# Token-expert layers of an eight-layer hybrid model: weights split once and kept in DRAM, spreading matrix by ScalarE, routing in halves, early tiles between late ones

## The chip, the cores and the metric

One core of one Trainium2 chip runs the whole kernel in one launch. The metric is the device time of one execution in microseconds; the median of the runs is compared. Engines are named as in the profile: PE (TensorE; PEld is its weight load), DVE (VectorE), ACT (ScalarE), POOL (GpSimd), SP (SyncE, which issues the DMAs).

## The reference

The model takes x of 4 x 512 tokens of 128 floats and adds eight layers to it, each on a layer norm of x: attention with a learned position bias, expert-choice experts, linear attention, experts again, a selective scan, the token-expert layer, a delta-rule layer, and the token-expert layer once more with the same weights. The token-expert layer is what this case is about:

```python
scores = jax.nn.sigmoid(x @ gate_weight.T)          # 32 experts in 4 groups
sc = scores + gate_bias                             # best 2 groups by their two best scores, best 6 experts in them
tw = tw / (tw.sum(-1, keepdims=True) + 1e-20) * 0.2 # weights of the 6
g, u = einsum('th,ehi->tei', x, w_gate), einsum('th,ehi->tei', x, w_up)
routed = sum over experts of cw * (silu(g) * u) @ w_down
shared = silu(x @ shared_w_gate) * (x @ shared_w_up) @ shared_w_down
anchor = one of 16 small experts, chosen by the best expert
out = routed + shared + 0.1 * anchor
```

All experts are computed for all tokens; the routing enters as a weight per token and expert. Inputs and outputs are float32.

## The kernel before

The kernel runs the layers one after the other, each as a block with five instruction streams. At a block's end all engines meet, so a layer starts when the one before is finished. The first layer is `layer_attention` (tag la), the sixth and eighth are `layer_moe_tokens` (tags lf and lh).

**The token layer.** The hidden columns of all experts stand side by side: 16 tiles of 128 columns for the 32 routed experts, 4 for the 16 anchors, 1 for the shared expert, which makes 21 tiles. The tokens are 4 chunks of 512. A unit is one tile of one chunk, so there are 84. Products are in fp32r, and to keep float32's accuracy weights and activations are split into a high and a low part, so each product is three matmuls (high by high, high by low, low by high).

*Head of the layer.* SP loads the raw weights in order anchors and shared, routed, then the down weights, which overwrite the raw gate weights and so wait until these are split. POOL builds a matrix `spread` of zeros and ones that spreads an expert's weight over its hidden columns (a memset and four affine selects), then splits the weights: three pieces of gate and up, then the down weights, each with a cast (L1554, L1563) and a subtraction (L1558, L1565). DVE normalises the tokens (L125), PE turns them (L136), ACT copies them out of PSUM twice (L1578, L1579), DVE subtracts the low part of the activations (L1626). PE makes the router's logits (L1735), ACT the sigmoid (L1581). Then DVE routes all 16 token tiles in one chain of small instructions (L1630 to L1689), of which nearly each waits for the one before. Meanwhile PE computes three early tiles, the last two anchor tiles and the shared one, for all chunks (12 units), and ACT keeps their silu and up parts (L1585, L1586). When the routing is done PE turns the routing weights (L1748), ACT copies them (L1589), and the main loop starts.

*Main loop.* For a late unit PE makes gate (three matmuls into bank 0 or 1), up (three into bank 2 or 3) and the spread weights (one into bank 4 or 5); ACT takes silu of the gate (L1611); DVE multiplies it by up (L1712) and by the spread weight (L1715); ACT rounds the result to its high part (L1596); POOL subtracts the low part (L1570); and two units later (LAG) PE makes the three down matmuls, which add into bank 6. An early unit has no gate and up matmuls: PE has one spread and three down matmuls in it (the shared tile three alone), while DVE, ACT and POOL have nearly the work of a late unit. The three early units stand at the end of each chunk. The rings of hidden values have 3 places. After each chunk ACT copies bank 6, PE turns it back (L1790) and DVE adds it to x (L1695).

**The attention layer.** It runs 16 groups (4 heads of one batch) in a software pipeline of 8 steps per group. PE, DVE (L434) and ACT work on every step; POOL copies the operands of group n into `stack` (L317) after it has copied the values of group n-2 (L325), which waits for PE's products of an older group. SP loads the position bias of each set of heads in turn (L268, L273), behind waits for DVE and for PE's scores.

## Time and profile before

| | us |
|---|---|
| median of 3 runs (1806.40 to 1813.23) | 1809.97 |
| the profiled execution | 1810.92 |
| its span, first to last instruction | 1807.4 |
| attention layer la, first to last DMA issue of the next layer | 7.4 to 344.7 |
| token layer lf | 1094.2 to 1347.9 |
| token layer lh | 1548.2 to 1801.9 |

PE is busy for 80% of the span, DVE for 68%, POOL for 42%, ACT for 40%; the DMA queue that SP feeds moved 31.21 MB in 6.6% of the 16 DMA engines' span. The rows that the prediction uses are in a section of their own below. Times are microseconds from the start of the span, and L numbers are lines of the kernel before.

### The profile page before, as it was taken

How to read it: one execution, taken by the hardware profiler on the slowest of the kernel's cores; microseconds unless marked ns; L12 is line 12 of the kernel's file. 1: busy time of each engine (PE TensorE's matmuls, PEld its weight loads, DVE VectorE, ACT ScalarE, POOL GpSimd, SP SyncE). 2: the span in 40 equal slices, each digit the busy share in tenths (PEclk: the TensorE clock that was granted, in tenths of full speed). 3: DMA queues.
4: the chain of work that ended last, by engine and by line, in shares of the span. 5: the costliest groups of instructions: out<-in, count | busy, mean ns of one | idle time of the engine just before them, and what ended most of it. 6: DMA issues, size and time to landing. Idle time of an engine off the chain costs nothing. (4 is left out here: it accounts for less than half of the span.)

```text
span 1807.4 us, 26498 instructions
## 1 busy us (share of the span) xinstructions
PE 1441.0 (80%) x9238; PEld 953.1 (53%) x9238; DVE 1232.8 (68%) x2834; ACT 727.1 (40%) x1218; POOL 751.0 (42%) x928
## 2 busy tenths in 40 slices
PE   4899999849965499785898886699974784669997
PEld 2333333428843278634665655476752583547775
DVE  5777777375567745667998997766667636876665
ACT  2277777511121212365443423344435111244443
POOL 3821220037510286003665656355561330635555
PEclk9599999969988699887999996799997797579999
DMA  1220100001100001100000003100000000310000
GB/s 52 64 80 19 59 2 1 25 0 36 35 11 23 2 24 37 27 1 0 1 1 1 1 1 61 30 1 1 0 7 1 0 1 1 61 30 1 1 1 24
DMA packets 39333, 32.70 MB, mean 18 GB/s; under 512 B 13856, under 2 KB 33392, under 8 KB 39216
## 3 DMA queue, kind: packets, MB, share of 16 engines
q1 hardware_dynamic: 39216, 31.21, 6.6%
q8 instruction: 65, 1.06, 0.2%
q14 instruction: 52, 0.43, 0.1%
HBM read 29.99 MB, written 1.21 MB: 17 GB/s over the span
## 5 line engine op out<-in xcount | busy, mean ns | idle before, releaser
L434 DVE CUSTOM_DVE_ANT_1 la_neg<-bank,la_table 128x512 f32<-128x512 f32 x256 | 166.5, 688 | 45.8 <-PE bank L525 45.2
L1712 DVE SCALAR_TENSOR_TENSOR xn<-xn,bank 128x512 f32<-128x512 f32 x144 | 99.0, 687 | 140.0 <-PE bank L1727 139.2
L1362 PEld LDWEIGHTS bank<-le_diag,le_dtxT 128*128 128x128 f32 x1024 | 126.3, 191 | 80.5 <-issue 59.1
L1362 PE MATMUL bank<-le_diag,le_dtxT 128*128 128x128 f32 x1024 | 141.8, 282 | 25.4 <-DVE le_h L1280 21.2
L1280 DVE TENSOR_TENSOR_SCAN le_h<-le_keep,bank 128x512 f32<-128x512 f32 x128 | 155.2, 1213 | 3.8 <-PE bank L1362 3.8
L1611 ACT ACTIVATE xn<-bank 128x512 f32<-128x512 f32 x144 | 86.1, 598 | 167.3 <-PE bank L1727 166.8
L1570 POOL TENSOR_TENSOR lf_h_low<-lf_wu,lf_h_high 128x512 fp32r<-128x512 f32 x84 | 109.2, 1301 | 90.4 <-ACT lf_h_high L1596 90.4
L1570 POOL TENSOR_TENSOR lh_h_low<-lh_wu,lh_h_high 128x512 fp32r<-128x512 f32 x84 | 109.3, 1301 | 90.3 <-ACT lh_h_high L1596 90.3
L1218 ACT ACTIVATE le_keep<-le_dt,le_A 128x512 f32<-128x512 f32 x128 | 92.1, 722 | 133.1 <-DVE le_h L1280 133.1
L361 ACT ACTIVATE la_probT<-bank 128x512 f32<-128x512 f32 x256 | 135.6, 605 | 13.4 <-PE bank L544 11.4
L1133 POOL TENSOR_TENSOR le_hc<-le_hc 128x512 f32<-128x512 f32 x64 | 81.0, 1266 | 101.7 <-DVE le_hc L1289 97.9
L1141 POOL TENSOR_TENSOR le_diag<-ident,le_bT 128x512 f32<-128x512 f32 x64 | 71.2, 1135 | 71.3 <-ACT le_bT L1205 70.4
L1289 DVE TENSOR_TENSOR le_hc<-le_h,bank 128x512 f32<-128x512 f32 x128 | 85.4, 668 | 9.4 <-issue 5.0
L325 POOL COPY la_v<-xn 128x128 f32<-128x128 f32 x16 | 4.8, 298 | 185.1 <-PE bank L555 185.1
L544 PE MATMUL bank<-la_bias_parts,la_spread 96*32 96x512 bf16 x1024 | 80.5, 392 | 0.0
L47 PE MATMUL bank<-ident 128*128 128x512 bf16 x100 | 29.9, 467 | 57.0 <-DVEq L738 40.4
L525 PE MATMUL bank<-la_qkT 48*128 48x512 bf16 x256 | 66.6, 412 | 5.5 <-DVE la_nmax L434 5.2
L555 PE MATMUL bank<-la_probT,la_v 128*32 128x512 f32 x512 | 67.5, 602 | 3.7 <-ACT la_mixT L374 3.5
L683 POOL TENSOR_SCALAR lb_pick<-lb_number,lb_own 128x128 bf16<-128x128 f32 x120 | 70.1, 610 | 0.8
L683 POOL TENSOR_SCALAR ld_pick<-ld_number,ld_own 128x128 bf16<-128x128 f32 x120 | 69.9, 609 | 0.8
L1924 POOL TENSOR_TENSOR lg_cT<-lg_aT,lg_masks 128x512 f32<-128x512 f32 x24 | 30.1, 1268 | 91.9 <-DVE lg_aT L2006 61.8
L1374 PE MATMUL bank<-le_hc,ident 128*128 128x512 f32 x128 | 65.7, 594 | 2.5 <-POOL le_hc L1133 2.5
(603 smaller groups left out, 3726.6 us busy)
## 6 DMA issues: line engine op xcount, KB each, us to landing
la_table<-la_scratch SPq DMA_DIRECT2D x4, 1792.0 KB, 7.1
la_bias_parts<-la_scratch_parts SPq DMA_DIRECT2D x12, 248.0 KB, 6.2
lb_w1s<-in_L_ffn_w_dram SPq DMA_DIRECT2D x8, 256.0 KB, 2.7
lb_w2s<-in_L_ffn_w_dram SPq DMA_DIRECT2D x8, 256.0 KB, 3.3
ld_w1s<-in_L_ffn_w_dram SPq DMA_DIRECT2D x8, 256.0 KB, 2.8
ld_w2s<-in_L_ffn_w_dram SPq DMA_DIRECT2D x8, 256.0 KB, 3.1
out_dram<-x SPq DMA_DIRECT2D x1, 1024.0 KB, 5.1
le_win<-in_L_attn_a_w_in_dram SPq DMA_DIRECT2D x1, 256.0 KB, 2.6
```

The source lines that it names most:

```text
L361: act.activation(probT[:, u % NPT, :], k.bank[RING1 + u % RING2][:], ACT.Exp).then_inc(exped, 1)
L434: dve.tensor_tensor_reduce(out=neg[:, u % 2, :].rearrange("p (c i) -> p c i", i=P), in0=k.bank[u % RING1][:].rearrange("p (c i) -> p c i", ...
L544: last = pe.matmul(k.bank[RING1 + u % RING2][i * CG:(i + 1) * CG, :], spread[:], bias_parts[:, n // B % 2, 2 * hp + e, w:w + T], start=Fal ...
L683: last = pool.tensor_scalar(pick[:, s, j, :], number[:], own[:, s, j:j + 1], None, ALU.is_equal)
L1133: pool.tensor_tensor(hc[:, p % PAIRS, 0, :], hc[:, p % PAIRS, 0, :], hc[:, p % PAIRS, 1, :], ALU.add).then_inc(paired, 1)
L1218: act.activation(keep[:, q % UN, :], dt_[:, c, g * G2 + bb, :], ACT.Exp, scale=A[:, c, n:n + 1]).then_inc(keep_ready, 1)
L1280: dve.tensor_tensor_scan(h[:, i, :], keep[:, i, :], k.bank[4 + q % 2][:], 0.0, ALU.mult, ALU.add).then_inc(scanned, 1)
L1289: dve.tensor_tensor(hc[:, p % PAIRS, n % 2, :], h[:, q % UN, :], k.bank[6 + n % 2][:], ALU.mult).then_inc(hc_ready, 1)
L1362: last = pe.matmul(k.bank[4 + q % 2][:, j * P:(j + 1) * P], dtxT[:, (g * G2 + bb) * TPB + j, c, :], diag[:, d % DIAGS, j, :], start=True, ...
L1570: pool.tensor_tensor(h_low[:, u % RING, :], hidden[:, u % RING, :], h_high[:, u % RING, :].bitcast(F32), ALU.subtract)\
L1611: act.activation(silu[:, v % 2, :], k.bank[v % 2][:, :], ACT.Silu).then_inc(silu_ready, 1)
L1712: dve.scalar_tensor_tensor(gated[:, n % 2, :], sl, 1.0 if t < ET else ALPHA, up, ALU.mult, ALU.mult).then_inc(gated_ready, 1)
```

## The change

One class `TokenWeights` is new. It declares six DRAM tensors, high and low parts of the gate, up and down weights, each 128 x 2688 floats (8.26 MB together). They are filled in the attention layer, in nine pieces of 7 tiles (896 columns): SP loads a piece, POOL casts it and subtracts, SP stores both parts. The pieces are loaded, split and stored in two slots; POOL splits piece i between groups, ahead of its copies for group n = 5 + i; SP issues the loads and stores behind its bias loads of the second, third and fourth set of heads, and waits for the last store before the layer ends.

Each token layer then loads the finished parts straight into their tiles, early columns first, the late columns in two halves, the down weights last, and splits nothing. POOL's only work in the head is the memset of `spread`; ACT fills it with four copies from the identity matrix, one ahead of its square root and three behind the copies of the turned tokens. PE turns the router's weights first and then runs 14 idle products, ahead of the turning of the tokens. DVE subtracts the low part of the activations from PSUM. The logits wait for each group of four turned tiles by itself.

The routing is a generator, called for 8 token tiles at a time with buffers of half the size. The first half runs ahead of the main loop; the second gives one small piece after each unit, up to unit 29, and its stack is turned at units 30 and 33. The order of tiles in a chunk is six late, one early, six late, one early, six late, the shared tile. LAG is 3 and the ring has 4 places. The hidden values and the chunk sums have buffers of their own.

The diff, cut to its core:

```diff
+class TokenWeights:
+    TILES_OF_PIECE = 7
+    PIECE = TILES_OF_PIECE * P
+    PIECES = 9
...
+        self.high = [nc.dram_tensor(f"token_{w}_high", [P, 3 * self.PIECE], F32) for w in ("gate", "up", "down")]
+        self.low = [nc.dram_tensor(f"token_{w}_low", [P, 3 * self.PIECE], F32) for w in ("gate", "up", "down")]
...
@@ layer_attention, SyncE @@
+            def load_piece(i):
+                if i >= 2:
+                    sp.wait_ge(piece_split, i - 1)
+                for place, source in weights.pieces[i]:
+                    sp.dma_start(place(split_raw[:, i % 2, :]), source).then_inc(piece_loaded[i % 2], 16)
+            def store_piece(i):
+                which, at = weights.place(i)
+                sp.wait_ge(piece_split, i + 1)
+                sp.dma_start(weights.high[which][:, at], split_high[:, i % 2, :].bitcast(F32)).then_inc(piece_stored[i % 2], 16)
+                sp.dma_start(weights.low[which][:, at], split_low[:, i % 2, :].bitcast(F32)).then_inc(piece_stored[i % 2], 16)
...
+                if g == 1:
+                    load_piece(0)
+                    load_piece(1)
+                if g >= 2:
+                    for i in (range(0, 4) if g == 2 else range(4, PIECES)):
+                        store_piece(i)
+                        if i + 2 < PIECES:
+                            load_piece(i + 2)
+            for slot in range(2):
+                sp.wait_ge(piece_stored[slot], 32 * len(range(slot, PIECES, 2)))
...
@@ layer_attention, GpSimd @@
+            def split_piece(i):
+                raw, high, low = split_raw[:, i % 2, :], split_high[:, i % 2, :], split_low[:, i % 2, :]
+                if weights.pad(i) is not None:
+                    link(pool.memset(weights.pad(i)(raw), 0.0))
+                pool.wait_ge(piece_loaded[i % 2], 16 * (loads_before(i) + len(weights.pieces[i])))
+                if i >= 2:
+                    pool.wait_ge(piece_stored[i % 2], 32 * (i // 2))
+                pool.tensor_copy(high, raw).then_inc(piece_high, 1)
+                pool.wait_ge(piece_high, i + 1)
+                pool.tensor_tensor(low, raw, high.bitcast(F32), ALU.subtract).then_inc(piece_split, 1)
...
+                if 5 <= n < 5 + PIECES:
+                    pool.wait_ge(v1_ready, n - 1)
+                    split_piece(n - 5)
...
@@ layer_moe_tokens @@
-    RING, LAG = 3, 2
+    GB, RING, LAG = 2, 4, 3
     U = B * TILES
+    HALF = NT // 2
+    ORDER = [t for i in range(EARLY) for t in (*range(i * LATE // EARLY, (i + 1) * LATE // EARLY), LATE + i)]
+    NO_WEIGHT = ORDER.index(TILES - 1)
...
+        SECOND_TURNS = {TILES + 9: 2, TILES + 12: 3}
+        SECOND_DUE = TILES + 8
...
@@ SyncE @@
+            for dst, src in ((wu_high, weights.high[1]), (wu_low, weights.low[1]), (wg_high, weights.high[0]), (wg_low, weights.low[0])):
+                sp.dma_start(dst[:, early_columns].bitcast(F32), src[:, early_columns]).then_inc(loaded_early, 16)
+            sp.dma_start(gb[:], gate_bias.partition_broadcast(P)).then_inc(loaded_gb, 16)
+            for columns in (slice(0, LATE // 2 * P), slice(LATE // 2 * P, LATE * P)):
+                for dst, src in ((wg_high, weights.high[0]), (wg_low, weights.low[0]), (wu_high, weights.high[1]), (wu_low, weights.low[1])):
+                    sp.dma_start(dst[:, columns].bitcast(F32), src[:, columns]).then_inc(loaded_late[columns.start > 0], 16)
+            for dst, src in ((wd_high, weights.high[2]), (wd_low, weights.low[2])):
+                sp.dma_start(dst[:].rearrange("p t d -> p (t d)").bitcast(F32), src[:, :]).then_inc(loaded_down, 16)
...
@@ GpSimd @@
-            link(pool.memset(wg[:, TILES * P - (P - SI):], 0.0))
-            link(pool.memset(wu[:, TILES * P - (P - SI):], 0.0))
...
-            for part in range(3):
-                v = spread[:, 0:ET * P].rearrange("r (e i) -> r e i", i=I)
-                link(pool.affine_select(out=v, in_=v, compare_op=ALU.not_equal, fill=1.0, base=-E * part,
-                                        pattern=[[-1, E], [0, I]], channel_multiplier=1))
...
-            for n, (t0, t1) in enumerate(((LATE, TILES), (0, LATE // 2), (LATE // 2, LATE))):
-                piece = slice(t0 * P, t1 * P)
-                if n == 1:
-                    pool.wait_ge(loaded_in, 16 * NI)
-                for raw, high in ((wu, wu_high), (wg, wg_high)):
-                    last = pool.tensor_copy(high[:, piece], raw[:, piece])
-                last.then_inc(high_ready, 1)
-                pool.wait_ge(high_ready, n + 1)
-                for raw, high, low in ((wu, wu_high, wu_low), (wg, wg_high, wg_low)):
-                    last = pool.tensor_tensor(low[:, piece], raw[:, piece], high[:, piece].bitcast(F32), ALU.subtract)
-                last.then_inc(low_ready, 1)
...
-            pool.wait_ge(loaded_w, 16 * NW)
-            pool.tensor_copy(wd_high[:], wd).then_inc(wd_ready, 1)
-            pool.wait_ge(wd_ready, 1)
-            pool.tensor_tensor(wd_low[:], wd, wd_high[:].bitcast(F32), ALU.subtract).then_inc(wd_ready, 1)
+            pool.memset(spread[:], 0.0).then_inc(cleared, 1)
...
@@ ScalarE @@
+            def make_spread(part):
+                n, columns = (E, slice(0, ET * P)) if part < 3 else (L, slice(ET * P, (ET + AT) * P))
+                rows = slice(E * part, E * part + n)
+                act.activation(spread[rows, columns].rearrange("r (e i) -> r e i", e=n), bcast(k.ident16[rows, E * part:E * part + 1], (1, n), (0, columns.stop // n - columns.start // n)), ACT.Copy)\
+                   .then_inc(spread_made, 1)
+            act.wait_ge(cleared, 1)
+            make_spread(0)
...
+            for part in range(1, 4):
+                make_spread(part)
...
+            for c in range(2):
+                copy_stackT(c)
+            for u in range(LAG):
+                silu(u)
...
@@ VectorE @@
-                dve.tensor_tensor(x_low[:, xg], k.xnT[:, xg], x_high[:, xg].bitcast(F32), ALU.subtract).then_inc(x_low_ready, 1)
-            dve.wait_ge(loaded_gw, 32)
+                dve.tensor_tensor(x_low[:, xg], k.bank[g][:], x_high[:, xg].bitcast(F32), ALU.subtract).then_inc(x_low_ready, 1)
...
+            def route(half):
+                tokens = slice(half * HALF, (half + 1) * HALF)
+                own = score[:, tokens, :]
...
+            for _ in route(0):
+                pass
+            second = route(1)
...
+                if u < SECOND_DUE:
+                    next(second, None)
+                if u == SECOND_DUE:
+                    for _ in second:
+                        pass
...
@@ TensorE @@
+            k.idle_products(pe, 14, 4)
...
+            pe.wait_ge(loaded_early, 64)
...
-            pe.wait_ge(stack_ready, 1)
-            for j in range(NT):
-                g, o = 6 + j // 8, j % 8
-                last = pe.transpose(k.bank[g][0:STK, :].bitcast(BF16)[:, o * P:(o + 1) * P], stack[:, j, :], k.ident16[:])
-                if o == 7:
-                    last.then_inc(stack_turned, 1)
-            pe.wait_ge(stackT_ready, 2)
-            pe.wait_ge(wd_ready, 2)
-            pe.wait_ge(early_kept, EARLY * B)
-            pe.wait_ge(spread_made, 7)
...
+            def turn_stack(c):
+                pe.wait_ge(stack_ready, c // 2 + 1)
+                if c == 2:
+                    pe.wait_ge(acc_used, 1)
+                if c == 3:
+                    pe.wait_ge(stackT_ready, 3)
+                for j in range(TPB):
+                    last = pe.transpose(turned_stack(c)[:, j * P:(j + 1) * P], stack[:, c * TPB + j, :], k.ident16[:])
+                last.then_inc(stack_turned, 1)
...
+            turn_stack(0)
+            turn_stack(1)
...
+                if u in SECOND_TURNS:
+                    turn_stack(SECOND_TURNS[u])
```

## Rows read from the trace of the kernel before

**Rows 1.** The page's first line.
```profile
span 1807.4 us, 26498 instructions
```

**Rows 2.** Timeline, lf's head: start, duration, engine, line, shapes, [idle <-releaser].
```profile
1094.20 0.33 SPq L1515 DMA_DIRECT2D lf_gw<-n_L_ffn_gate_weight_dram  x1
...
1097.46 6.68 POOL L1540 TENSOR_SCALAR_AFFINE_SELECT lf_spread<-lf_spread 128x2048 bf16<-128x2048 bf16 x3
...
1100.18 9.51 DVE L125 TENSOR_SCALAR xn<-x,lf_mv,lf_rstd 128x128 f32<-128x128 f32 x16
...
1111.49 1.45 POOL L1554 CAST lf_wu_high<-lf_wu 128x1152 fp32r<-128x1152 f32 x1 [3.16 <-DMA lf_wu<-in_L_ffn_w_up_dram]
```

**Rows 3.** Timeline of lg, the layer after lf: normalisation.
```profile
1353.18 4.39 DVE L125 TENSOR_SCALAR xn<-x,lg_mv,lg_rstd 128x128 f32<-128x128 f32 x16
```

**Rows 4.** Timeline of lf's routing on DVE, with POOL.
```profile
1119.42 1.68 DVE L1630 TENSOR_TENSOR xnT<-lf_score,lf_gb 128x512 f32<-128x512 f32 x1 [1.37 <-ACT lf_score L1581]
...
1123.47 2.74 POOL L1558 TENSOR_TENSOR lf_wu_low<-lf_wu,lf_wu_high 128x1152 fp32r<-128x1152 f32 x1
...
1123.70 2.66 DVE L1637 TENSOR_TENSOR lf_t<-lf_hi 128x128 f32<-128x128 f32 x1
...
1128.97 0.28 DVE L1639 TENSOR_TENSOR lf_hi<-lf_hi 128x128 f32<-128x128 f32 x1
...
1151.91 0.43 DVE L1689 CAST lf_stack<-xnT 128x512 bf16<-128x512 f32 x1
```

**Rows 5.** Timeline of lf, ahead of the main loop.
```profile
1138.16 0.59 ACT L1586 ACTIVATE lf_up_e<-bank 128x512 f32<-128x512 f32 x1
...
1153.53 1.94 ACT L1589 ACTIVATE lf_stackT<-bank 112x1024 bf16<-112x1024 bf16 x2 [14.77 <-PE bank L1748]
...
1155.52 0.79 PE L1725 MATMUL bank<-lf_x_high,lf_wg_high 128*128 128x512 f32 x1 [1.17 <-ACT lf_stackT L1589]
```

**Rows 6.** Windows: length, PE, PEld, DVE, ACT, POOL busy, clock, DMA.
```profile
1155.50:1160.30 4.80, 4.78 (x11) 3.50 (x12) 1.38 (x2) 0.68 (x2) 0.00 (x0) 0.50 0.00 0
```

**Rows 7.** Timeline of PE: first matmuls of two late units.
```profile
1163.39 0.39 PE L1725 MATMUL bank<-lf_x_high,lf_wg_high 128*128 128x512 f32 x1
...
1165.68 0.39 PE L1725 MATMUL bank<-lf_x_high,lf_wg_high 128*128 128x512 f32 x1
```

**Rows 8.** Timeline of PE: ends of chunk 0 and loop.
```profile
1197.80 0.39 PE L1772 MATMUL bank<-lf_stackT,lf_spread 112*128 112x512 bf16 x1
...
1202.62 0.39 PE L1725 MATMUL bank<-lf_x_high,lf_wg_high 128*128 128x512 f32 x1
...
1337.64 0.39 PE L1772 MATMUL bank<-lf_stackT,lf_spread 112*128 112x512 bf16 x1
...
1345.05 0.51 PE L1783 MATMUL bank<-lf_h_low,lf_wd_high 128*128 128x512 f32 x1 [0.26 <-POOL lf_h_low L1570]
```

**Rows 9.** Timeline of lh: its main loop's first matmul.
```profile
1609.55 0.79 PE L1725 MATMUL bank<-lh_x_high,lh_wg_high 128*128 128x512 f32 x1 [1.17 <-ACT lh_stackT L1589]
```

**Rows 10.** L1712 by form: min/median/max ns, starts, shape.
```profile
L1712 DVE SCALAR_TENSOR_TENSOR xn<-xn,bank x144: 686/687/689, 1158.6 to 1790.9; 128x512 f32<-128x512 f32 x144
L1712 DVE SCALAR_TENSOR_TENSOR xn<-lf_silu_e,lf_up_e x8: 961/1006/1052, 1198.4 to 1339.9; 128x512 f32<-128x512 f32 x8
```

**Rows 11.** Attention layer: timelines, and L434 from its tile's view.
```profile
132.71 2.91 POOL L317 COPY la_stack<-la_part 128x128 bf16<-128x128 bf16 x12
...
144.13 1.25 SPq L273 DMA_DIRECT2D la_bias_parts<-la_scratch_parts  x3
...
161.59 0.62 PE L512 MATMUL bank<-ident,la_stack 128*128 128x128 bf16 x8
...
L434 DVE CUSTOM_DVE_ANT_1 la_neg<-bank,la_table x256: 677/687/693, 58.0 to 318.4; 128x512 f32<-128x512 f32 x128
```

**Rows 12.** DMAs: KB and landing; GB/s in 40 slices, 1100 to 1112.
```profile
la_table<-la_scratch SPq DMA_DIRECT2D x1, 1792.0 KB, 7.3
...
GB/s 165 24 0 85 218 154 164 304 355 266 225 218 218 218 218 218 198 225 222 225 205 205 236 225 215 218 218 218 218 218 218 215 208 181 137 96 24 0 0 0
```

More of the change, by code:

```diff
@@ L243, in group_at, with loads_before @@
             return n if r == 0 and 0 <= n < GROUPS else None
+        weights = k.token_weights
+        PIECES = weights.PIECES
+        def loads_before(i):
+            return sum(len(weights.pieces[j]) for j in range(i % 2, i, 2))
         block = ctx.enter_context(nc.Block())
@@ L1667, in _ @@
-            dve.memset(only1[:, :, 1:8], LOW)
-            dve.tensor_copy(only1[:, :, 0], best[:, :, 0])
-            link(dve.memset(best[:, :, TOPK:8], LOW))
-            for j in range(NT):
-                dve.match_replace(work[:, j, :], best[:, j, :], masked[:, j, :], HIT)
-                last = dve.match_replace(work1[:, j, :], only1[:, j, :], masked[:, j, :], HIT)
-            link(last)
-            w8 = work.rearrange("p j (g e) -> p (j g) e", e=GE)
-            w18 = work1.rearrange("p j (g e) -> p (j g) e", e=GE)
@@ L1697, in _ @@
             for u in range(U):
[L1698 removed]
+                c, s, t = place_of(u)
                 if t < LATE:
[L1700 to L1701 removed]
+                    v = late_before(u)
+                    sl, up = silu_l[:, v % GB, :], k.bank[GB + v % GB][:]
                     dve.wait_ge(silu_ready, v + 1)
@@ L1775, in down @@
             def down(u):
-                c, t = tile_of(u)
+                c, s, t = place_of(u)
+                if u == 0:
+                    pe.wait_ge(loaded_down, 32)
+                    pe.wait_ge(stackT_ready, 2)
                 pe.wait_ge(h_high_ready, u + 1)
-                if c and t == 0:
+                if c and s == 0:
                     pe.wait_ge(acc_copied, c)
-                pe.matmul(k.bank[6][:], wd_high[:, t, :], h_high[:, u % RING, :], start=(t == 0), stop=False)
+                pe.matmul(k.bank[6][:], wd_high[:, t, :], h_high[:, u % RING, :], start=(s == 0), stop=False)
@@ L1796, in _ @@
                     down(u - LAG)
-                    c, t = tile_of(u - LAG)
-                    if c and t == 1:
+                    c, s, t = place_of(u - LAG)
+                    if c and s == 1:
                         turn_acc(c - 1)
+                if u in SECOND_TURNS:
+                    turn_stack(SECOND_TURNS[u])
             for u in range(U - LAG, U):
```

371 lines of the change are left out of this document (213 added, 158 removed).

## The prediction

> **What bounds the kernel now.** The page's first line comes first: the profiled execution has a span of 1807.4 us [rows 1] and a time of 1810.92, 0.95 above the median of the runs. The sum is made against 1810.92. About 0.5% (9 us) is what a measurement can tell from no change. The layers run one after the other, so I read the two token layers and the attention layer by their timelines; whatever a layer saves or loses goes into the end one to one. Each token layer takes 253.7 us (1094.20 to 1347.89 for lf; lh the same within 0.1).
>
> The token layer falls into two parts. The head, from the first DMA at 1094.20 to the main loop's first matmul at 1155.52 [rows 2, 5], takes 61.3 us, and PE is not its bound. The early units are kept at 1138.75; then PE waits until the routing chain on DVE ends at 1152.34 and ACT has copied the stack [rows 4, 5]. The routing started at 1119.42, late, since the normalisation of 16 tiles took 9.51 us beside POOL's affine selects, against 4.39 in the next layer [rows 2, 3]. lh has the same head: 1548.2 to 1609.55 [rows 9].
>
> The main loop, 1155.52 to the last down matmul at about 1345.4 [rows 5, 8], takes 189.9 us and is bound by PE. Two late units stand 2.29 us apart and hold ten matmuls, so 0.229 us for one [rows 7]. The loop has 72 x 6 gate and up, 80 spread and 84 x 3 down matmuls, 764 in all: 175.0 us, with some 1.1 for turning the sums back 176.1. The other 13.8 are three losses. The first 4.8 us run at a clock of 0.50, that is 1.2 GHz of 2.4, after PE's wait [rows 6]: 2.4 lost. At each chunk's end eleven matmuls (2.5 us) take 4.82, from 1197.80 to 1202.62, as PE waits for POOL's low parts [rows 8]: 2.3 lost, three times. At the loop's end 17 matmuls (3.9 us) take 7.76 [rows 8]: 3.9 lost. Together 13.2.
>
> **The change part by part, for one token layer, as time after its start.**
>
> *POOL out of the head.* The affine selects (6.68 for three) and all casts and subtractions go; a memset stays. The normalisation falls from 9.51 to 4.39 [rows 2, 3]; it starts at +6.0 and ends at +10.4 instead of +15.5. From the old end (1109.69) to the routing's first instruction (1119.42) it was 9.7 us, mostly logits [rows 2, 4]. These now start group by group, but ACT gets three spreading copies in front of the sigmoid. A copy of 2048 columns is worth two of the 1024-column ones, 1.94 us [rows 5], a short one 0.5: 4.4 us of ACT, most of which lies beside the logits. I take 8.3 us (6 to 11), so routing starts at +18.7 instead of +25.2. The fourth copy stands ahead of the square root, which is wanted at about +5; it ends about then. I cost it at nothing; without that cover 2 us. The idle products of PE end before the last token tile is there; nothing behind them waits for more than the tiles; at worst 2 us.
>
> *Routing in halves.* The chain took 32.9 us for 16 tiles [rows 4]. Some 8 of it are waits beside POOL: L1637 took 2.66 us beside a POOL subtraction of 2.74, its equal behind it 0.28 [rows 4]. Of the clean 25, the comparisons of groups (about 4 us of tiny instructions) don't shrink, the rest about halves: 15 (13 to 18). First half done at +34 instead of +58.1.
>
> *Early units.* They wait for logits and early weights, which land by then, and for ACT's silu of the first, behind the sigmoid. Before, the routing's start and the last kept unit stood 19.3 us apart (1119.42 to 1138.75) [rows 4, 5]; I take 17.6, as the first four now need no cold start. They are kept at +36.3, so here the early units end last, not the routing; PE turns eight stack tiles beside it. The loop starts at +36.4 instead of +61.3: **24.9 us** gained (18 to 28).
>
> *Main loop.* The clock loss goes (PE is busy up to the loop): 2.4. Early units now stand between late ones: PE spends 0.9 us in one, the other engines more, but over two units (3.2 us of PE) they fit, and LAG 3 gives one unit, 2.29 us, of slack. I take the 6.9 us of the chunk ends as gone. Of the 3.9 at the end 2.3 stay, since a late and an early unit remain to pass through DVE, ACT and POOL. New: 1.0 for turning the second half's stack, and 2.0 for the pieces of the second routing (0 to 13). These are 15 us of DVE in 25 units, 0.6 a unit, beside two multiplications of 0.69 [rows 10]: 2.0 of 2.29. Queued behind a piece are the next unit's multiplications, which have the slack of LAG. The gain is 13.8 - 2.3 - 1.0 - 2.0 = **8.5** (2 to 12).
>
> *Weights by DMA.* A layer loads 8.26 MB in place of 4.1, in order of need. The attention layer's bias, 1.84 MB from DRAM in long rows, lands in 7.3 us [rows 12]: 8.26 MB take 33 us at that rate, latency counted each time, and at the 218 GB/s of the short rows of lf's own weights [rows 12] 38. The late half is wanted at +36 and is there before +20; the down weights, last in SP's queue, are wanted three units later, at about +43. I cost it at nothing; at half the short-row rate the down weights come at +76, 33 us late.
>
> *Attention layer.* POOL gets nine splits of 896 columns: a cast of 1.45 x 896/1152 = 1.13 and a subtraction of 2.74 x 896/1152 = 2.13 [rows 2, 4], 29 us in all, in a stretch where it idles for most of a group. Group 7's stack was copied at 132.71 and turned at 161.59 [rows 11]. Now POOL waits there for piece 2, which SP loads only after its bias parts at 144.13 [rows 11]; with about 5 us of load, 3.3 of split and 2.9 of copies the stack is ready near 156, in front of 161.6. Group 11 (piece 6) is the same. DVE's L434 lies within 677 to 693 ns in all 256 [rows 11], also while POOL worked, as it reads PSUM and one tile. I take 2 us (0 to 31).
>
> *The port.* A DVE instruction on SBUF alone waits beside POOL: L1637's row, and L1712 with two SBUF inputs at 1006 ns against 687 with one from PSUM [rows 4, 10]. The Trainium skill's SBUF — State Buffer, section "SBUF: two separate sides", says that DVE and GpSimd take their shared port pair as an exclusive lock for a whole instruction, and the other fully blocks. L1637's row agrees. By that rule each piece of the second routing can wait for a whole h_low of POOL, which the sum by the rows does not charge.
>
> **Sum.** 2 x (24.9 + 8.5) = 66.8 gained, 2 lost: 1810.9 - 64.8 = 1746.1 against the profiled execution, so **1745** against the median.
>
> **The rivals.**
> 1. *The second routing slows the loop.* For: the two rows on the port. If a piece waits out a whole POOL subtraction of 512 columns, 2.74 x 512/1152 = 1.2 us [rows 4], DVE needs 2 x 0.69 + 0.6 + 1.2 = 3.2 us a unit against 2.29, 0.9 more, in 25 units: 23 us a layer. Against: POOL's subtraction runs mostly beside the PSUM multiplications, and a late DVE meets it less. Half of it, 12 a layer (2 of them in the sum), gives 1745 + 2 x 10 = 1765. Chance 0.17.
> 2. *The down weights come late.* For: they are the last of sixteen DMAs in one queue. At two thirds of the short-row rate, 145 GB/s, they land at +58, 15 us late in each layer: 1775. Against: 218 GB/s even in short rows [rows 12]. Chance 0.08.
> 3. *More is hidden.* No loss for the second routing or the attention layer, and the loop starts 3 us sooner: 1745 - 2 x 5 - 2 = 1733. Chance 0.10.
> 4. *Slower: POOL and DVE lock each other out in both places.* If DVE stands still for all of the nine splits, 29 us, and waits out two POOL instructions a unit in the second routing (1.4 + 0.6 + 2.4 = 4.4 us against 2.29, 53 us a layer), that is 29 + 106 = 135 against a gain of 67: 1878. It decides from 67 us of waits. For: L1637. Against: L434's narrow spread, and POOL has one instruction a unit. The lock of the Trainium skill's page is this mechanism. Chance 0.05.
> The forecast has 0.60.
>
> **How the numbers follow.** The forecast's own range is 1732 to 1760. 1730 to 1774 takes in the forecast, rival 3 at its middle and rival 1 up to three quarters of its full price, about 8 in 10, and leaves out rival 4 and most of rival 2. Faster by over 0.5% are all cases but rival 4 and a mixture of 1 and 2 with a stalled attention layer: 0.94; same 0.02, slower 0.04.
>
> **What would show it.** In lf: normalisation near 4.4 us; routing from about +19 to +34; the loop's first matmul near +36 with a clock of 1.00; no waits for low parts at the early units; units 2.29 apart also up to unit 25; a layer of about 220 us. In la: L434 as before, and the next layer's first DMA within 3 us of 344.7. I am wrong if the first down matmul waits for a DMA, if units up to 25 stand 2.6 or more apart, or if PE waits in la for `stack`.

## The result, and the profile after

The changed kernel takes 1751.92 us (median of 4 runs, 1743.05 to 1753.96), the one before 1808.24 (4 runs): ratio 0.9675, 95% interval 0.9636 to 0.9714. The forecast was 1745 (1730 to 1774). The profiled execution took 1753.96; its span is on the page's first line, against 1807.4 [rows 1].

```profile
span 1752.3 us, 26727 instructions
```

Each layer's length, from its first DMA to that of the next layer (the output's DMA for lh), shows where the 55.1 us of span came from:

| | before | after | saved | forecast |
|---|---|---|---|---|
| la ends at | 344.72 | 350.78 | -6.1 | -2 |
| lf | 253.69 | 223.66 | 30.0 | 33.4 |
| lg | 200.34 | 199.78 | 0.6 | 0 |
| lh | 253.63 | 222.29 | 31.3 | 33.4 |

The four layers between la and lf took 0.8 us longer together.

Inside lf the main loop's first matmul moved from +61.3 to +38.7 (lh: +37.3), and the loop to the layer's end shrank from 192.4 (lh 192.3) to 185.0. The forecast said 24.9 and 8.5; 22.6 (lh 24.1) and 7.4 (lh 7.3) came.

The timeline of lf's head (start, duration, engine, line; the layer starts at 1101.07) answers [rows 2, 4, 5]:

```profile
1105.72 1.28 ACT L158 ACT_TABLE_LOAD   x1
...
1107.55 4.20 DVE L170 TENSOR_SCALAR xn<-x,lf_mv,lf_rstd 128x128 f32<-128x128 f32 x16
...
1112.30 3.66 PE L1845 MATMUL bank<-lf_gwT,xnT 128*128 128x32 f32 x32
...
1113.72 4.49 ACT L1637 ACTIVATE lf_spread<-ident 32x2048 bf16<-32x2048 bf16 x3
1118.23 1.28 ACT L1652 ACT_TABLE_LOAD   x1
1119.52 0.60 ACT L1652 ACTIVATE lf_score<-bank 128x512 f32<-128x512 f32 x1
...
1120.26 0.42 DVE L1713 TENSOR_TENSOR xnT<-lf_score,lf_gb 128x256 f32<-128x256 f32 x1 [5.84 <-ACT lf_score L1652]
...
1122.57 0.74 PE L1833 MATMUL bank<-lf_x_high,lf_wu_high 128*128 128x512 f32 x1 [2.18 <-ACT lf_up_e L1657]
...
1136.33 0.29 DVE L1788 CAST lf_stack<-xnT 128x256 bf16<-128x256 f32 x1
...
1139.75 0.47 PE L1833 MATMUL bank<-lf_x_high,lf_wg_high 128*128 128x512 f32 x1 [0.82 <-ACT lf_up_e L1657]
```

The normalisation takes 4.20 in place of 9.51, and the first half's routing 16.4 (1120.26 to 1136.62). But ACT finishes its three spreading copies at 1118.21, when the logits have been ready since 1116.0, so the sigmoid starts 3.5 us late. The table load in front of it costs 1.28 of those; the load at 1105.72 holds the square root, whose input was ready at 1105.73, by as much. PE then waits 2.18 us for ACT's early unit, and the three matmuls of a bank, at 0.39 to 0.40 each in the timeline when the clock is high, go to 0.63 behind it. In lh no table load stands ahead of the square root, and the normalisation ends at +9.4 instead of +10.7; PE's wait for ACT there is 3.65 us, and the clock is 0.50 behind it too.

The loop starts at full clock. This window is that of [rows 6], counted from the new first matmul (length, busy times, then granted clock and DMA):

```profile
1139.70:1144.50 4.80, 4.75 (x22) 3.41 (x22) 2.88 (x5) 2.62 (x5) 0.00 (x0) 1.00 0.00 0
```

1.00 is 2.4 GHz, where it was 0.50. The loop's end answers the last two of [rows 8]:

```profile
1316.91 0.39 PE L1881 MATMUL bank<-lf_stackT,lf_spread 112*128 112x512 bf16 x1
...
1321.90 0.50 PE L1905 MATMUL bank<-lf_h_low,lf_wd_high 128*128 128x512 f32 x1 [0.28 <-POOL lf_h_low L1629]
```

The first row is now the last spreading product of the loop, that of the last late unit: 16 matmuls from there to the last down matmul, in 4.99 us. The row of the kernel before is that of an early unit, with another one still to come: 17 matmuls, in 7.41. At 0.229 from one to the next, 3.75 us were lost, and 1.55 are. PE's waits for the low parts in these stretches say the same (total, times, longest; before, then after):

```profile
PE bank L1783 <- POOL lf_h_low L1570: 2.4, 5, 0.7
```
```profile
PE bank L1905 <- POOL lf_h_low L1629: 0.9, 2, 0.6
```

In the attention layer POOL now waits for a late load, and behind that DVE stands still (timelines of SP, POOL, DVE and PE in order of time; the stretch of [rows 11]):

```profile
148.53 3.14 SPq L309 DMA_DIRECT2D la_split_raw<-L_ffn_shared_w_gate_dram  x1
...
155.16 0.93 POOL L391 CAST la_split_high<-la_split_raw 128x896 fp32r<-128x896 f32 x1 [5.88 <-DMA la_split_raw<-L_ffn_shared_w_gate_dram]
...
155.20 0.93 DVE L535 CAST la_stack<-la_nmax 128x8 bf16<-128x8 f32 x1
...
156.17 2.12 POOL L393 TENSOR_TENSOR la_split_low<-la_split_raw,la_split_high 128x896 fp32r<-128x896 f32 x1
...
156.37 1.96 DVE L537 CAST la_stack<-la_mrest 128x8 bf16<-128x8 f32 x1
...
158.24 2.89 POOL L409 COPY la_stack<-la_part 128x128 bf16<-128x128 bf16 x12
...
166.01 1.03 PE L604 MATMUL bank<-ident,la_stack 128*128 128x128 bf16 x8
```

The two casts of 8 columns take 0.93 and 1.96 us; they end with POOL's cast (156.09) and subtraction (158.29). In the next group, without such a meeting, they take 0.19 and 0.18 (DVE's timeline):

```profile
167.45 0.19 DVE L535 CAST la_stack<-la_nmax 128x8 bf16<-128x8 f32 x1
...
167.88 0.18 DVE L537 CAST la_stack<-la_mrest 128x8 bf16<-128x8 f32 x1
```

PE waits for DVE (of 150 to 168: total, times, longest), and the clock falls behind that wait:

```profile
PE bank L617 <- DVE la_nmax L526: 1.7, 2, 1.5
```
```profile
160.30:166.90 6.60, 6.60 (x41) 1.76 (x40) 2.55 (x9) 2.77 (x5) 0.83 (x4) 0.50 0.59 136
```

The maxima on DVE, L526, stand 0.1 us earlier than in the kernel before up to 154, 1.5 later at 160 and 4.8 later from 170 on: 1.6 by the wait, and 3.3, half of 6.6 us, by the clock. A second meeting at group 11 (226.15, again 1.97 us) adds 1.3 without a fall of the clock. Group 7's stack, ready at 161.13, was in time: PE turned it at 166.01 and is shown no wait for it.

### The profile page after: what moved, and what is told of

The parts are those of the page before. It is cut to its first block and busy times, and to the rows that moved or that the text cites. A ratio compares the mean times of both kernels' runs of the same rounds, so it can differ in the third digit from the quotient of the medians.

```text
span 1752.3 us, 26727 instructions
## 1 busy us (share of the span) xinstructions
PE 1434.9 (82%) x9266; PEld 944.5 (54%) x9266; DVE 1214.2 (69%) x2940; ACT 741.8 (42%) x1232; POOL 708.3 (40%) x907
## 5 line engine op out<-in xcount | busy, mean ns | idle before, releaser
L526 DVE CUSTOM_DVE_ANT_1 la_neg<-bank,la_table 128x512 f32<-128x512 f32 x256 | 166.3, 688 | 47.8 <-PE bank L617 47.2
L1629 POOL TENSOR_TENSOR lf_h_low<-lf_hidden,lf_h_high 128x512 fp32r<-128x512 f32 x84 | 110.5, 1317 | 107.6 <-ACT lf_h_high L1674 106.1
L1629 POOL TENSOR_TENSOR lh_h_low<-lh_hidden,lh_h_high 128x512 fp32r<-128x512 f32 x84 | 110.4, 1316 | 106.1 <-ACT lh_h_high L1674 105.6
L453 ACT ACTIVATE la_probT<-bank 128x512 f32<-128x512 f32 x256 | 135.6, 605 | 14.2 <-PE bank L636 12.2
L48 PE MATMUL bank<-ident 128*128 128x512 bf16 x128 | 39.1, 474 | 57.0 <-DVEq L830 40.4
```

Of the source, the lines that this page charges most:

```text
L453: act.activation(probT[:, u % NPT, :], k.bank[RING1 + u % RING2][:], ACT.Exp).then_inc(exped, 1)
L526: dve.tensor_tensor_reduce(out=neg[:, u % 2, :].rearrange("p (c i) -> p c i", i=P), in0=k.bank[u % RING1][:].rearrange("p (c i) -> p c i", ...
L1629: pool.tensor_tensor(h_low[:, u % RING, :], hidden[:, u % RING, :], h_high[:, u % RING, :].bitcast(F32), ALU.subtract)\
```

## The experiments

Twelve kernels ran: four undo one part of the change, two shorten the loop's lag, six arrange work in another way. Times are medians, with the ratio to the kernel before and its interval; layer lengths come from each profile.

**1. The idle products.** Edit:

```
-            k.idle_products(pe, 14, 4)
             norm.tensor(pe)
```

> The changed kernel (profiled 1754.0) with the 14 idle products of PE ahead of the normalised tiles taken out of both token layers. Theory: they hold the clock high for the logits (3.66 us in the changed kernel, 7.01 in the one before), and delay the first transposes by some 0.4. Without them the logits take 7 us again, each token layer is 3 us longer (223.7 to 226.7) and the time is 1760. Rival: ACT's spreading copies hold the sigmoid until 3.5 us after the logits anyway, so the longer logits fill a wait that exists; token layers 223.7 (within 0.7), time 1754.

1751.68 us (0.9667, 0.9648 to 0.9685); lf 222.3, lh 222.7. The rival holds. In lh the logits are slow again and nothing comes later, since ACT is still making the spreading matrix (PE's and ACT's timelines of lh, which starts at 1522.75):

```profile
1533.14 6.88 PE L1844 MATMUL bank<-lh_gwT,xnT 128*128 128x32 f32 x32
```
```profile
1534.49 4.49 ACT L1637 ACTIVATE lh_spread<-ident 32x2048 bf16<-32x2048 bf16 x3
1538.99 1.28 ACT L1652 ACT_TABLE_LOAD   x1
1540.29 0.60 ACT L1652 ACTIVATE lh_score<-bank 128x512 f32<-128x512 f32 x1
```

The sigmoid stands at +17.5 against +17.1 with fast logits. As placed, the idle products are worth nothing.

**2. The order of the tiles.** Edit:

```
-    ORDER = [t for i in range(EARLY) for t in (*range(i * LATE // EARLY, (i + 1) * LATE // EARLY), LATE + i)]
+    ORDER = list(range(TILES))
```

> The changed kernel with the early tiles at the end of every chunk, as before, instead of between late ones. Theory of the prediction: at each of three chunk ends PE waits 2.3 us for low parts, so a token layer grows by 6.9 (223.7 to 230.6) and the time is 1768. Rival: most of these waits went with the deeper rings and the longer lag, which stay; then a layer grows by 0 to 2.5 and the time is 1754 to 1759.

1756.14 us (0.9693, 0.9677 to 0.9709); the loop takes 188.0 in both layers, 3.0 more than 185.0. The layers are only 225.5 and 223.7, because the heads, which the edit doesn't touch, came out 1.2 and 1.5 us shorter in this profile. The truth lies just above the rival's bound, at less than half of the 6.9 that the prediction gave to the order. And 1.1 of the 3.0 lies at the loop's end, where PE waits 2.0 us for low parts in place of 0.9.

**3. The lag, and both.** Edits: `RING, LAG = 3, 2` in place of `4, 3`; and with it the order of experiment 2.

> The changed kernel with the lag of 2 and the ring of 3 of the kernel before, the early tiles still between late ones. The loop (first late matmul to the layer's end) takes 185.0 in the changed kernel and 188.0 with the early tiles at the chunks' ends. Theory: the order and the longer lag both work on the same waits for low parts, and each does part of it; with the short lag an early unit leaves too little time wherever it stands: loop 188 to 190, time 1758 to 1763. Rival: the order does it all (as the prediction costed it) and the lag nothing: loop 185 to 186, time 1752 to 1755.

1763.91 us (0.9739, 0.9722 to 0.9756); loop 190.3 in both layers, 5.3 more.

> Both undone: lag 2, ring 3, early tiles at the chunks' ends. Theory: the loop goes back to that of the kernel before without its slow start and with the second routing in it: 192.4 - 2.4 + 1.5 for the pieces + 1.0 for turning the second stack = 192.5, against 185.0; time 1767. Rival: the rest of the change (the stack in quarters, the sums' own tiles, DMA instead of POOL's splits) also moved the loop; then it stays below 190 and the time below 1762.

1771.79 us (0.9779, 0.9758 to 0.9801); loop 194.4 and 193.0, 8.0 to 9.4 more. Both theories hold in kind, and both loops came out a little longer than they said (188 to 190, and 192.5): the 3.0 and the 5.3 add up. The waits of PE's weight loads for POOL's low parts, in lf from 1160 to 1320, show the same. First the changed kernel, then order undone, lag undone, both:

```profile
PEld bank L1905 <- POOL lf_h_low L1629: 0.2, 1, 0.2
```
```profile
PEld bank L1905 <- POOL lf_h_low L1629: 3.6, 4, 1.4
```
```profile
PEld bank L1905 <- POOL lf_h_low L1629: 8.0, 11, 0.9
```
```profile
PEld bank L1905 <- POOL lf_h_low L1629: 9.3, 9, 1.5
```

The columns are us in total, times, longest. An early unit gives PE 0.9 us of work; with a lag of two units its low part is late wherever the unit stands.

**4. The whole routing ahead of the loop.** Edit:

```
-            second = route(1)
+            for _ in route(1):
+                pass
+            second = iter(())
```

> The changed kernel with both halves of the routing ahead of the loop, so none of it in the loop. Theory: the second half takes the 16.4 us of the first; it would end at about +52 of the layer, the loop starts 13.3 later than the present +38.7, and is shorter by what the second half costs in it, 1.5 us (0.5 to 3). A token layer takes 223.7 + 13.3 - 1.5 = 235.5, the time is 1777. Rival 1 of the prediction: the second half costs the loop 7 to 13 us; then the loop's 185.0 us fall to 172 to 178, the layer takes 224 to 230 and the time is 1754 to 1766.

1770.49 us (0.9778, 0.9762 to 0.9794); lf 233.2, lh 232.5. The time falls between the theory's 1777 and the 1766 at which its rival ends, and the picture of both was wrong: the loop's first matmul stays at +38.6 in lf, and the wait stands inside the loop, 9.6 us of PE for DVE. So the second half's price is read from DVE's first multiplication of the loop to the layer's end. In this kernel (lf from 1096.62 to 1329.78) and in the changed one (1101.07 to 1324.73):

```profile
1148.02 0.29 DVE L1788 CAST lf_stack<-xnT 128x256 bf16<-128x256 f32 x1
1148.23 0.68 DVE L1817 SCALAR_TENSOR_TENSOR xn<-xn,bank 128x512 f32<-128x512 f32 x1
```
```profile
1141.52 0.69 DVE L1815 SCALAR_TENSOR_TENSOR xn<-xn,bank 128x512 f32<-128x512 f32 x1 [4.89 <-PE bank L1835]
```

181.55 without the second half in the loop, 183.21 with it: 1.7 us (in lh 182.1 and 183.3: 1.1). The prediction had 2.0. The difference is not a clean one: at its start PE stood in the third late unit here and in the second there, and the clock is 0.50 behind PE's wait here. But the changed kernel's own waits of PE for DVE give the same size (lf from 1140 to 1320, all before 1169):

```profile
PE bank L1881 <- DVE lf_hidden L1818: 1.0, 2, 0.8
...
PE bank L1833 <- DVE xn L1815: 0.3, 1, 0.3
```

With the steps from one matmul to the next around them these three places lose 1.85 us. Rival 1 of the prediction, 12 us, is gone.

**5. The spreading matrix by POOL again.** Edit:

```
-            pool.memset(spread[:], 0.0).then_inc(cleared, 1)
...
+            link(pool.memset(spread[:], 0.0))
+            for part in range(4):
...
+                link(pool.affine_select(out=v, in_=v, compare_op=ALU.not_equal, fill=1.0, base=-E * part, pattern=[[-1, n], [0, lanes]], channel_multiplier=1))
+            pool.sem_inc(spread_made, 4)
```
(and ACT's four copies taken out)

> The changed kernel with the spreading matrix made by POOL's affine selects as before, not by ACT. Theory: POOL's 7.4 us of selects stretch the normalisation again (4.2 us to 8 or 9.5), but ACT's four copies and the table load behind the first of them no longer hold the square root (1.3) and the sigmoid (3.5 behind the logits), and PE's wait of 2.2 us at the third early unit goes with its slow matmuls. The two come out even: sigmoid within 1.5 us of the present +18.4, token layer 222 to 226, time 1751 to 1758. Rival, as the prediction had it: ACT's copies are nearly free and POOL's selects cost 5.1 us of normalisation; then a token layer takes 229 and the time is 1764.

1753.17 us (0.9673, 0.9657 to 0.9689); lf 222.8, lh 222.9. The theory holds: the two come out even. lf starts at 1101.64 here (POOL's, then DVE's timeline):

```profile
1104.48 7.59 POOL L1629 TENSOR_SCALAR_AFFINE_SELECT lf_spread<-lf_spread 128x2048 bf16<-128x2048 bf16 x4
...
1107.20 7.75 DVE L170 TENSOR_SCALAR xn<-x,lf_mv,lf_rstd 128x128 f32<-128x128 f32 x16
...
1120.53 0.42 DVE L1715 TENSOR_TENSOR xnT<-lf_score,lf_gb 128x256 f32<-128x256 f32 x1 [2.56 <-ACT lf_score L1654]
```

The selects stretch the normalisation by 3.55 us, and the routing starts at +18.9, against +19.2 with ACT's copies (in lh +19.1 against +17.8, where the changed kernel has no table load ahead of the square root). What DVE gained by leaving POOL, the sigmoid lost to ACT's copies.

**6. ACT's copies in other places.** Edit:

```
+        warm = sb("warm", [P, 1])
...
+            act.activation(warm[:], k.eps[:], ACT.Sqrt)
             act.wait_ge(cleared, 1)
             make_spread(0)
             norm.scalar_sqrt(act)
+            make_spread(1)
...
-            for part in range(1, 4):
-                make_spread(part)
+            make_spread(2)
             act.wait_ge(logits_ready, 1)
...
+            make_spread(3)
```
(the last behind the early units)

> The changed kernel with ACT's spreading copies in other places: a first square root of one column that loads the table ahead of the first copy, the second copy behind the normalisation's square root, the third behind the copies of the turned tiles, the fourth behind the early units. Theory: sigmoid 4 us earlier (+18.4 to +14.4), so the third early unit no longer waits 2.2 us for ACT and its clock stays high; the early units end at +34 instead of +37.2, the loop starts 4.4 us earlier, a token layer takes 219.3, the time is 1745. Rival: the early units are bound by PE from +14.7 at a low clock anyway, and the sigmoid is not on their path: loop starts within 1 us of +38.7, time 1752 to 1754.

1746.42 us (0.9645, 0.9623 to 0.9668); both layers 219.9. The theory holds in outcome: lf's loop starts at +35.1 (1133.32, the layer from 1098.21), 3.6 earlier. The sigmoid came at +15.5 and not at +14.4, since the logits ran slowly in lf here (5.50). PE's wait of 2.2 for ACT's early units is gone in lf; among the waits of 1112 to 1133, ACT now waits for PE:

```profile
ACT lf_silu_e L1658 <- PE bank L1839: 4.5, 12, 0.8
...
ACT lf_score L1654 <- PE bank L1849: 1.0, 1, 1.0
```

In lh, where the logits are fast, the third copy and the table load still hold the sigmoid, at +16.2, and of PE's 3.65 us of waiting 2.50 are left (PE's timeline):

```profile
1537.38 0.50 PE L1837 MATMUL bank<-lh_x_high,lh_wu_high 128*128 128x512 f32 x1 [2.50 <-ACT lh_up_e L1659]
```

The loop starts at +34.9 in lh. Both starts are below all those of profiles whose heads were not edited (+35.7 and more), so the gain is not their scatter, though the two intervals of the time overlap.

**7. The wait filled.** Edit: ten idle products of PE ahead of the third early unit.

> The changed kernel with 10 idle products of PE between the second and the third early unit, where PE waits 2.2 us for ACT. The wait stays, only PE is busy in it. Theory: of what the late sigmoid costs, a part is the wait and a part the low clock behind it: the third and fourth unit at 2.7 and 1.8 us instead of 1.41. With the clock kept high the early units end 1.7 us earlier, a token layer takes 222, the time is 1750.5. Rival: the granted clock falls for another reason than this wait, or the idle products hold the third unit back as long as the clock gives: layer within 0.5 of 223.7, time 1754.

1752.95 us (0.9673, 0.965 to 0.9696): no gain that can be measured. lf is 221.8, lh 223.3. In lh the gate weight landed late, PE waited 4.72 us for it, and the 14 idle products behind it held the transposes. The stretch by itself is plain. From the third early unit to the turning of the stack it was 15.7 us in both layers of the changed kernel (1122.57 to 1138.32 in lf) and is 14.2 in both here (1123.09 to 1137.32). The two windows, the changed kernel's first:

```profile
1122.50:1138.30 15.80, 15.73 (x60) 11.94 (x61) 12.84 (x84) 10.78 (x21) 0.00 (x0) 0.89 0.17 71
```
```profile
1122.50:1137.30 14.80, 14.80 (x64) 10.81 (x62) 13.28 (x88) 11.30 (x22) 0.00 (x0) 1.00 0.22 92
```

The granted clock is 0.89 over the stretch behind a PE that waited, 1.00 behind one that was kept busy, and that is 1.5 us, beside the 2.2 of the wait itself. In the other profiles the stretch takes one of the same two times: 15.7 to 15.8 us where the clock fell at the third unit, 14.1 to 14.3 where it was 1.00. It doesn't fall behind each such wait: in lf of experiments 1 and 2 PE waited 2.3 us and the clock stayed at 1.00.

**8. The splits one group later.** Edit:

```
+            SPLIT_AT = [5, 6, *range(8, 8 + PIECES - 2)]
...
-                if 5 <= n < 5 + PIECES:
+                if n in SPLIT_AT:
                     pool.wait_ge(v1_ready, n - 1)
-                    split_piece(n - 5)
+                    split_piece(SPLIT_AT.index(n))
```

> The changed kernel with the splits of weight pieces 2 to 8 one group later in the attention layer, so POOL asks for each piece 16 us after its load at the earliest. The same work on every engine. Theory: the 6.1 us that this layer lost are two waits of POOL for loads that SP issues late, in order behind its waits for the bias (5.9 us at piece 2, 5.5 at piece 6), which make the stacks of groups 7 and 11 late; they go, the next layer starts 0.5 to 1 us after the 344.7 of the kernel before, and the time is 1748. Rival: POOL's splits themselves (3.1 us in front of each stack) or the transfers beside the scores cost it; then the layer's loss stays at 4 to 6 us and the time at 1754.

1748.36 us (0.9658, 0.9639 to 0.9676). By the time alone, 3.6 us with overlapping intervals, this can't be told from the changed kernel; the trace shows it. The loss goes, as the theory said, and the rival is out, since the same splits and transfers are still there. The maxima keep one distance to those of the kernel before from the 40th to the 250th (-2.7 us; the start came earlier in this execution). With the splits where the change put them, that distance grew at groups 7 and 11 together by 6.1, 4.5, 5.1, 1.6, 5.8, 4.2, 5.3, 5.1 and 7.6 us in nine profiles (the changed kernel, experiments 1, 2, 4, 5, the two of 3, 6 and 7). But the theory's reason, late stacks, falls: by the trace shown above nobody waited for one. The edit also moved the splits. They stand right behind the group's start now, and DVE's casts run alone (POOL's, then DVE's timeline):

```profile
163.09 0.93 POOL L391 CAST la_split_high<-la_split_raw 128x896 fp32r<-128x896 f32 x1
164.10 2.10 POOL L393 TENSOR_TENSOR la_split_low<-la_split_raw,la_split_high 128x896 fp32r<-128x896 f32 x1
...
168.95 0.19 DVE L536 CAST la_stack<-la_nmax 128x8 bf16<-128x8 f32 x1
```

The size of the loss follows the clock. Group 7 cost 4.9 us where the clock was 0.50 from 160.2 to 166.8 (the changed kernel), 2.9 where it was 0.74 (experiment 5) and 1.3 where it stayed at 1.00 (experiment 4).

**9. The splits put where DVE casts.** This tells the two reasons apart: nothing late, but meetings. Edit, on top of experiment 8:

```
-                if n in SPLIT_AT:
-                    pool.wait_ge(v1_ready, n - 1)
-                    split_piece(SPLIT_AT.index(n))
                 if n < GROUPS:
...
                     last.then_inc(stacked, 1)
+                if n in SPLIT_AT:
+                    pool.wait_ge(stacked, n + 1)
+                    split_piece(SPLIT_AT.index(n))
...
+                link(pool.tensor_copy(high, raw))
                 pool.tensor_copy(high, raw).then_inc(piece_high, 1)
```

> The kernel with the splits a group later, but each split behind the stack copies of its group instead of ahead of them, and its cast done twice. No load is waited for, and every stack is ready 3 us earlier than in the kernel with the splits a group later. What changes is that POOL's subtraction of 2.1 us now runs from about 5 to 7 us behind the group's start, where DVE makes its three short casts of the maxima (0.19, 0.17 and 0.18 us, at 6.1 behind the start). Theory, formed from the trace of the changed kernel, against the one told for the later splits: what the attention layer lost was not late stacks but DVE held by POOL's split in these casts (1.96 us in place of 0.18), with PE's clock falling behind it in some executions. Then each of 9 pieces costs 1 us, and up to 5 where the clock falls: the attention layer 8 to 40 us longer, time 1756 to 1788. Rival (late stacks, or loads): nothing is late, the layer loses less than 1 us, time 1748.

1750.23 us (0.9669, 0.9649 to 0.969). In time this can't be told from experiment 8, and both forecasts missed. In the trace the meeting is plain, in all nine groups with a split (0.92 to 1.17 in place of 0.19); here the first behind group 7 (POOL's, then DVE's timeline):

```profile
172.01 2.08 POOL L394 TENSOR_TENSOR la_split_low<-la_split_raw,la_split_high 128x896 fp32r<-128x896 f32 x1
...
173.01 1.12 DVE L537 CAST la_stack<-la_nmax 128x8 bf16<-128x8 f32 x1
```

The cast ends with the subtraction again. The maxima fall back by 2.3 us from the first of these groups to the last (+0.95 to +3.2 against the kernel before), 0.25 for each meeting, and the clock stays at 1.00. So holding DVE does cost this layer time though nothing is late; but of a hold of 0.75 to 1.0 most is slack, and the expected 8 us and more did not come. In the changed kernel two casts in a row were held for 2.5.

**10. Copies and splits moved together, and a finer wait.** Edits 6 and 8 with 10 idle products; then also PE's first late units waiting for the early unit whose banks they take.

> Spreading copies in the other places, 10 idle products instead of 14, and the splits a group later, together. Theory: 8.8 to 11 us from the token layers and 5.5 from the attention layer add up: 1738 to 1740. Rival: only one of the two gives anything: 1745 to 1748.

1741.33 us (0.9615, 0.9597 to 0.9633). lf 218.7, lh 219.1; the distance in the attention layer stays at -0.3 from the 40th maximum on. The two gains add up (5.5 and 3.6 alone, 10.6 together against 1751.92; forecast 1738 to 1740), with the shorter row of idle products as a third edit that was not run by itself. This version beats both kernels.

> The kernel with the spreading copies and the splits in other places and 10 idle products, and one wait made finer: the first late unit waits for the early unit whose banks it takes (the 11th), not for the last one. Theory: PE's 0.82 us of waiting between the turned stack and the first late matmul goes, in both layers; 1.6 us less, time 1739.7. Rival: the loop's start is then bound by the stack, which ACT copies only behind its last early unit, and the gain is under 0.5 in all: 1741.

1742.74 us (0.9614, 0.9597 to 0.9632). The rival holds: PE's first late matmul comes at once behind the stack's turning, and the spreading product then waits for the stack's copy, which ACT makes behind its last early unit and the last spreading copy.

```profile
1134.13 0.38 PE L1886 MATMUL bank<-lf_stackT,lf_spread 112*128 112x512 bf16 x1 [1.14 <-ACT lf_stackT L1673]
```

0.82 us of waiting went and 1.14 came.

## Why the prediction was right, and where its terms were off

**The head: right in its chain, 2.3 us short in lf (0.8 in lh).** The term that was mis-sized is that of the early units. From the routing's start to the last kept unit the forecast took 17.6 us, "as the first four now need no cold start"; it was 19.3 in both layers, as before. The cold start moved: PE waits at the third unit for ACT (2.18 us in lf, 3.65 in lh), and the clock is 0.50 behind that; in lf the first unit ran at 0.50 as well. Experiment 7 keeps PE busy in this wait, and there it is 17.8 in both layers.

Ahead of that the sum held, in part by luck. In lf the normalisation ended at +10.7 (forecast +10.4) and the routing started at +19.2 (+18.7). The fourth copy was not free ("I cost it at nothing"): it lay over the table load, so that 1.28 us of load came into the square root's path; in lh, without this load, the routing started at +17.8. And "most of which lies beside the logits" holds only for half of the 4.49: the warm logits ended 2.2 us before the copies. The 8.3 us from the normalisation's end to the routing came out at 8.5 by another sum than thought: faster logits and a later sigmoid. Experiments 1, 5 and 6 show this. Fast logits alone and ACT's spreading alone give nothing, since either only moves the time to the other; with the copies moved, both layers gain.

**The routing in halves.** 16.4 us against 15 (13 to 18). The early units still ended last, as said, at +38.5 instead of +36.3.

**The loop: 7.4 against 8.5 (lh 7.3).** The slow start of 2.4 went (clock 1.00). The end lost 2.2 less (3.75 to 1.55; forecast 1.6 less). The second routing cost 1.7 and 1.1 by experiment 4, 1.85 by the trace, forecast 2.0. The 6.9 of the chunk ends went, but not through the order alone: the lag with its ring does 5.3 and the order 3.0 of the 8.0 to 9.4 that both are worth, the loop's end included. The prediction named the lag only as slack for the early unit. Two things made the sum too high. It took off 13.8 us of losses where those that it names are 13.2. And undisturbed late units (those 2.2 to 2.4 apart) stand 2.316 us apart on average, where it was 2.295: by an estimate, 0.02 over 72 units, that is 1.5 us a layer. What lengthens them no experiment shows.

**The port.** The lock that the prediction weighed is there. The same instruction on 64 columns ahead of the loop, and in it beside POOL's subtraction of 1.3 us (min/median/max ns of two, then first and last start):

```profile
L1721 DVE TENSOR_TENSOR lf_lo<-lf_lo x2: 218/768/1319, 1121.4 to 1146.6; 128x64 f32<-128x64 f32 x2
```

218 ns and 1319 ns. This agrees with the Trainium skill's SBUF — State Buffer, section "SBUF: two separate sides", by which the engine that comes second to the shared ports stands still for the whole of the other's instruction. In the loop it did not grow to the rival's time, since few pieces meet the subtraction: of the 94 instructions of the second half, 8 took over 0.15 us longer than the same ones of the first, 4.4 us of DVE in each layer, of which PE lost 1.85. Late units stand 2.29 to 2.33 apart, near the forecast's 2.29; across the first early tile of the first chunk it is 4.31, behind two such pieces in a row, and 3.3 in the later chunks.

**The weights: nothing, as forecast.** SP issued the last at 1109.40; it took 17.8 us to land, so near 1127; the first down matmul ran at 1146.10. The down weights had 19 us to spare, and rival 2 is out by that much. The 8.26 MB took 26 us from the layer's start, where the prediction had costed 33 to 38.

**The attention layer: 6.1 against 2, and the step that failed.** The prediction looked for a late stack at group 7 and found none, rightly in the end: ready at 161.1 rather than 156, as SP issued the last of three loads only at 148.53, yet in time for PE. Then it checked the port for L434 alone ("as it reads PSUM and one tile"); L526 did stay at 688 ns. The three short instructions between the maxima work on SBUF alone, and a split that waited for its load fell on them. So the prediction's rival 4 had the right mechanism, in a place where it named the nine splits as a whole: not 29 us, but two meetings of 2.5 and 1.9 us, of which 1.6 and 1.3 reach PE, and 3.3 from the clock. One of the signs that the prediction named failed with it: the next layer's first DMA was to come within 3 us of 344.7, and came at 350.78. Experiments 8 and 9 show the meetings and their removal. Why the clock falls behind the same wait in one execution and not in another stays open.

The terms short add up: 4.1 in the attention layer, 2.3 + 0.8 in the heads, 1.1 + 1.2 in the loops, 9.5 in all; 64.8 - 9.5 = 55.3 against 55.1 of span.

## What to carry to other kernels

When work is moved off one engine onto another that "has time", write down what stands behind it in the new engine's queue, down to the table load: here four copies on ACT cost the sigmoid what they had spared DVE, and only placing them between waits made the gain. Work that waits for a late load lands where nobody planned it: look which SBUF-only instructions of DVE stand there, however short, and ask for the data one period later. And a lag of one more unit, with one more place in the ring, was worth more than the clever order.

## What was not expected of the hardware

Behind a wait of PE of 1.5 us in the attention layer the clock was 0.50 for 6.6 us in the changed kernel. Behind 0.9 us it fell in experiment 5 and stayed at 1.00 in experiment 4, and behind 1.2 us it stayed at 1.00 in experiment 1: the length of the wait alone does not tell. The 1.28 us load of ACT's tables stood behind the copy that was queued ahead of the square root, at 1105.72 in the changed kernel, and at the layer's start where no copy stood before it (1101.66, experiment 5). And heads with the same instructions differ: in profiles whose heads were not edited (the changed kernel and experiments 2, 3, 8 and 9) the loop started between +35.7 and +39.1. Of this 1.5 us is the clock at the third early unit, low or not; the rest stays open.
